# Moving the layer-norm work of the chunk two ahead one 128-token step sooner, in the two 16-head attention stages of a fused four-layer kernel

## The reference

```
L0: x += g * attn16x64(ln(x)*(1+sc)+sh);   x += g * gelu_mlp(ln(x)*(1+sc)+sh)
L1: x += g * attn16x16(rms(x)*w*(1+sc)+sh) # q, k normed per head, 3d rope
    x += g * swiglu_mlp(...)
L2: x += g * attn16x16(ln(x)*(1+sc)+sh)    # biases, rope over 64 positions
    x += g * gelu_mlp(...);  x += gelu(v)*tanh(g) @ W
L3: x += low-rank products with gelu
norm in front of an attention or MLP:
  m = mean(x); d = x - m                   (L1: no mean, d = x)
  v = mean(d*d); h = d / sqrt(v + eps) * (1 + scale) + shift
attention, within each sequence of 64 tokens:
  softmax(q k^T / sqrt(head size)) v @ W_out + b_out
```

## Time and profile before

| | us |
|---|---|
| median of three runs (2367.0 to 2367.68) | 2367.48 |
| the profiled execution's own time | 2364.86 |
| its span, first to last instruction | 2363.1 |
| TensorE matmul busy | 2005.7 (85%) |
| VectorE busy | 1455.1 (62%) |
| ScalarE busy | 968.7 (41%) |
| GpSimd busy | 835.4 (35%) |
| idle of PE ahead of the q, k projection L1378, in the page's groups | 78.3, of it 63.6 until HL (L588) |

### The profile page before, as it was taken

The page is one execution under the profiler, slowest core; times in us unless marked ns, Lnnn a source line. Parts: engine busy times, 40 slices in busy tenths (PEclk is TensorE's granted clock), DMA queues, the critical chain, the costliest instruction groups (busy, mean ns, idle before and its releaser), DMA issues. The chain is left out here.

```text
span 2363.1 us, 41380 instructions
## 1 busy us (share of the span) xinstructions
PE 2005.7 (85%) x15274; PEld 1565.9 (66%) x15274; DVE 1455.1 (62%) x2120; ACT 968.7 (41%) x1594; POOL 835.4 (35%) x759
## 2 busy tenths in 40 slices
PE   4829999999999799867787679997877877998998
PEld 4618878878887577646565567774655656777775
DVE  1236655656566455468888856775777774554554
ACT  0024434434444566534454433332333345664332
POOL 0041111211011344456665723345656572443000
PEclk9959999999999999978999989998998999999999
DMA  7120000000000100010000000001000000000001
GB/s 301 55 74 2 2 2 1 1 2 1 1 1 10 49 0 0 0 41 2 0 0 0 1 25 0 0 1 36 1 0 0 0 2 27 0 0 32 5 0 72
DMA packets 19519, 44.28 MB, mean 19 GB/s; under 512 B 3200, under 2 KB 11200, under 8 KB 18176
## 3 DMA queue, kind: packets, MB, share of 16 engines
q1 hardware_dynamic: 19392, 42.48, 5.1%
HBM read 36.18 MB, written 6.29 MB: 18 GB/s over the span
## 5 line engine op out<-in xcount | busy, mean ns | idle before, releaser
L1223 DVE TENSOR_TENSOR Glb<-Gfb,Ghb 128x512 fp32r<-128x512 f32 x176 | 168.2, 964 | 101.6 <-ACT Ghb L1176 100.0
L523 POOL TENSOR_TENSOR Tm<-Dv,MOD 128x512 f32<-128x512 f32 x96 | 111.3, 1179 | 298.6 <-DVE Dv L580 208.0
L633 PE MATMUL bank<-HH,W1b 128*128 128x512 f32 x448 | 183.8, 410 | 13.2 <-PEq L1493 6.9
L633 PE MATMUL O<-Ghb,W2b 128*128 128x512 f32 x352 | 144.1, 409 | 54.0 <-DVE Glb L1223 52.4
L634 PE MATMUL bank<-HL,W1b 128*128 128x512 f32 x448 | 177.2, 396 | 0.0
L635 PE MATMUL bank<-HH,W1b 128*128 128x512 f32 x448 | 176.9, 395 | 0.0
L1378 PE MATMUL bank<-WQKa,HH 128*128 128x512 f32 x256 | 101.4, 483 | 78.3 <-DVE HL L588 63.6
L653 POOL TENSOR_TENSOR spare<-RT 128x1 f32<-128x1 f32 x48 | 9.5, 197 | 446.0 <-DVE RT L644 446.0
L512 POOL TENSOR_TENSOR XS<-Tm 128x512 f32<-128x512 f32 x48 | 70.5, 1469 | 245.6 <-ACT Tm L478 245.6
L635 PE MATMUL O<-Ghb,W2b 128*128 128x512 f32 x352 | 138.4, 393 | 0.0
L634 PE MATMUL O<-Glb,W2b 128*128 128x512 f32 x352 | 137.8, 392 | 0.0
(11 more groups left out here) (244 smaller groups left out, 5470.0 us busy)
## 6 DMA issues: line engine op xcount, KB each, us to landing
w<-l_w_dram SPq DMA_DIRECT2D x4, 2048.0 KB, 26.7
wm<-w_mods_dram SPq DMA_DIRECT2D x6, 768.0 KB, 12.1
X<-xT_dram SPq DMA_DIRECT2D x4, 1024.0 KB, 36.3
out_dram<-XO SPq DMA_DIRECT2D x8, 512.0 KB, 2.7
W2b_f<-l_w_dram SPq DMA_DIRECT2D x11, 256.0 KB, 5.0
WQK_f<-l_wqk_dram SPq DMA_DIRECT2D x8, 256.0 KB, 7.1
W1b_0f<-l_w_dram SPq DMA_DIRECT2D x8, 256.0 KB, 3.5
b2r<-l_b2r_dram SPq DMA_DIRECT2D x1, 1024.0 KB, 7.7
```

The source lines that it names most:

```text
L523: nc.gpsimd.tensor_tensor(Tm[:, k].rearrange("p (b t) -> p b t", t=T), Dv[:, k].rearrange("p (b t) -> p b t", t=T), m, ALU.mult).then_inc( ...
L633: nc.tensor.matmul(out, w_lo_ap, x_hi, start=first, stop=False)
L1223: nc.vector.tensor_tensor(Gl[m % gb][:], gf, Gh[m % gb][:].bitcast(F32), ALU.subtract).then_inc(g_lo.h, 1)
```

## The change

In `attention12` alone, on all engines. For chunk c + 2: mean, d, square and ss stand at t = 1 (mean behind weights-times-v on PE, d behind OT on DVE); sqh and sql at t = 2; var (behind S) and v at t = 3; rstd, norm and pool_h at the end of t = 3, norm behind OT on DVE; HH and HL at the end of the tail, HL behind OL and ahead of the residual. Chunk 1, for which the norm starts ahead of the loop, gets pool_h, HH and HL at the end of the first step. The last chunk no longer has its own places: the next stage's chunk 0 is finished in chunk 6's tail, and its chunk 1 goes up to v at t = 3 of chunk 7, in the usual bank (`nf.var_bank` goes). No instruction of the engines is added or taken away, no DMA is touched, and the number of waits stays but for two that fall with the special cases.

```diff
@@ TensorE
-                            if not more:                      # in project_rest
-                                pe.wait_ge(s_sub.h, s_sub.at(NT))
-                                nf.var_bank = S2[:, 0, :]
-                                nf.pe_var(pe, 1)
...
                                 last.then_inc(s_ready.h, 1)
-                            if t == 2:
+                            if t == 3:
                                 f, cc = early(fr, nf, c, more)
-                                f.pe_mean(pe, cc)
-                            if tail and more:
-                                f, cc = early(fr, nf, c - 1, more)
                                 f.pe_var(pe, cc)
...
                                 weigh(pe, tt - 1, prev)
+                            if t == 1:
+                                f, cc = early(fr, nf, c, more)
+                                f.pe_mean(pe, cc)
                             if tail:
                                 pe.wait_ge(ot_hi.h, ot_hi.at(tt - 2)); pe.wait_ge(ot_lo.h, ot_lo.at(tt - 2))
-                                f, cc = early(fr, nf, c - 1, max(more, 1))
-                                pe.wait_ge(f_v.h, f.at(f_v, cc + 1 if more else 1))
+                                f, cc = early(fr, nf, c - 1, more)
+                                pe.wait_ge(f_v.h, f.at(f_v, cc + 1))
                                 project(1, 0)
@@ ScalarE
-                            if t == (1 if more else 3):       # ahead of q_t, oh and exp
-                                f, cc, pp = late(fr, nf, c, p, more)
-                                f.act_hh(act, cc, pp)
-                            if more and t == 3:
-                                f, cc = early(fr, nf, c, more)
-                                f.act_sqh(act, cc)
-                            if not more and tail:
-                                nf.act_sqh(act, 1)
...
-                            if t == (2 if more else 3):       # at the step's end
-                                f, cc = early(fr, nf, c, more)
+                            f, cc = early(fr, nf, c - 1 if tail else c, more)
+                            if t == 1:
                                 f.act_square(act, cc)
-                            if more == 2 and tail:
-                                fr.act_rstd(act, c + 1)
-                            if not more and t == 1:
-                                nf.act_rstd(act, 0)
+                            if t == 2:
+                                f.act_sqh(act, cc)
+                            if t == 3 and more:
+                                f.act_rstd(act, cc)
+                            if tail and more:
+                                f.act_hh(act, cc, 1 - p)
...
                         step(0, 0, 0, 2, first=True)
+                        fr.act_hh(act, 1, 1)
@@ VectorE
-                            if tail and more:                 # behind S less its maximum
-                                f, cc = early(fr, nf, c - 1, more)
+                            if t == 3:
+                                f, cc = early(fr, nf, c, more)
                                 f.dve_v(dve, cc)
...
-                            if t == (1 if more else 3):       # behind spread_k and ol
-                                f, cc, pp = late(fr, nf, c, p, more)
-                                f.dve_hl(dve, cc, pp)
-                            if t == (2 if more else 3):
-                                f, cc = early(fr, nf, c, more)
-                                f.dve_d(dve, cc)
...
                             if tail:
                                 ol(tt - 1, prev)
-                            if more == 2 and tail:
-                                fr.dve_norm(dve, c + 1)
-                            if not more and t == 1:
-                                nf.dve_norm(dve, 0)
+                            f, cc = early(fr, nf, c - 1 if tail else c, more)
+                            if t == 1:
+                                f.dve_d(dve, cc)
+                            if t == 3 and more:
+                                f.dve_norm(dve, cc)
+                            if tail and more:
+                                f.dve_hl(dve, cc, 1 - p)
...
-                            if not more:                      # in residual
-                                nf.var_bank = S2[:, 0, :]
-                                nf.dve_v(dve, 1)
...
                         fr.dve_norm(dve, 1)
+                        fr.dve_hl(dve, 1, 1)
@@ GpSimd, behind pool_rope
-                            if not more and t == 2:
-                                nf.pool_h(pool, 0, 0)
-                            f, cc = early(fr, nf, c, more)
-                            if t == (2 if more else 3):
+                            f, cc = early(fr, nf, c - 1 if tail else c, more)
+                            if first:
+                                fr.pool_h(pool, 1, 1)
+                            if t == 1:
                                 f.pool_ss(pool, cc)
+                            if t == 2:
+                                f.pool_sql(pool, cc)
                             if t == 3 and more:
-                                f.pool_sql(pool, cc)
-                            if not more and tail:
-                                nf.pool_sql(pool, 1)
-                            if more == 2 and t == 0:
-                                fr.pool_h(pool, c + 1, 1 - p)
+                                f.pool_h(pool, cc, p)
```

More of the change, by code:

```diff
@@ L1692, in _ @@
                     def _(dve):
-                        nf.var_bank = O2[:, 1, :]
                         dve.wait_ge(step_p.h, step_p.at(2 * TL))
```

## The result

| | before, us | changed, us |
|---|---|---|
| median (lowest to highest) | 2367.24 (2361.16 to 2367.68), 4 runs | 2333.93 (2330.18 to 2336.78), 4 runs |
| the profiled execution's own time | 2364.86 | 2335.44 |
| its span | 2363.1 | 2333.6 |
| mean granted TensorE clock | 0.946 | 0.955 |

The ratio is 0.9858, with a 95% interval of 0.9836 to 0.988: 33 us faster. The prediction was 46 us less for the profiled execution and a median of 2321. The two profiled executions differ by 29.4 us.

What follows compares the result with a forecast made beforehand. PE's waits for HL in t = 1 and long tails bound it, plain steps DVE (L1) or PE (L2). Periods -15.6 and -22.2, starts +3 and +1, ends -7.5 and -5 gave -46.3 us: 2318.6, median 2321, range 2308 to 2335.

Steps and rivals of the forecast that it cites:

- t = 1: Projection no longer waits for HL: L1's step 7.1 us, 6.5 less; L2's 8.3 us, 5.1 less.
- t = 2: Step loses the mean and the low clock: -1.9 us in L2, -0.8 in L1.
- t = 3 and tail: Taken as one piece, longer by the norm ahead of the tail's maximum: +4.4 us in L1, +2.7 in L2.
- HH and HL free: At the tail's end HH and HL cost nothing, since DVE has 4.5 us and more before t = 1's work.
- The clock: Half clock behind the tail's new PE stall of about 4 us costs 1.5 us a chunk, bounds 0 and 5.25.
- Six periods: Chunks of 40.9 us in L1 and 38.6 in L2 against means 43.5 and 42.3: -15.6 and -22.2 us.
- The starts: Each stage's first chunk pays the longer tail, its wait only moved: +3 us in L1, +1 in L2.
- Ends: Last chunk loses the next stage's norm, PE's longest KB waits, HH and HL: -7.5 us in L1, -5 in L2.
- B: Rival: the norm in t = 3 meets POOL's rope and stretches, 1.9 us a chunk, 23 us worse, 2344; chance 0.15.
- the signs that the prediction had named for being wrong: t = 1 keeps over 10 us, tail piece grows over 7 us, or t = 3's norm operations exceed 1 us.
- A: Rival: the tail's stall leaves PE's clock up, no clock loss, 18 us better, 2303; chance 0.14.
- C: Rival: tail's stall puts half clock on projections and S; slower beyond 5.4 us a period, 2380 at 6.5; chance 0.06.

Runs made afterwards that it cites:

- the third experiment: The changed kernel with HH and HL alone put back into t = 1, norm and pool_h staying early: 2354.11 us.
- the filled kernel: The changed kernel with repeated output-projection matmuls in PE's idle time in each tail, four more in L1 and three more in L2: 2337.85 us.
- the PT experiment: The changed kernel, but in L1's tails ACT copies PT ahead of the two root operations of SS: 2347.91 us.
- L2 alone: The change in the second 16-head stage only, the first built as in the kernel before: 2343.54 us.
- The first experiment: The changed kernel with norm and pool_h of chunk 1 ahead of the first step in both 16-head stages: 2320.81 us.
- The early half: Run alone on the kernel before: the pieces up to v one step sooner; rstd, norm, pool_h, HH and HL where they were: 2355.82 us.

## Why the prediction was right, and where its terms were off

The sign, the mechanism and the range held, the range by little: 2333.93 lies 1 us inside the forecast's own bound of 2335. The forecast of 2321 was 13 us under the measured median, and that it wasn't further off is in part luck, since L2's periods won 1.9 us more than their term. Step by step:

- *t = 1.* Right. No projection in the loop waits for HL; 7.8 (7.1 predicted) and 8.27 (8.3) us. The 0.7 in L1 is the plain step of the earlier trace rows, read at PE, where single steps scatter.
- *t = 2.* 6.8 in L2, as predicted; 7.8 in L1, the same misreading.
- *t = 3 and tail.* 9.37 + 16.15 against 7.11 + 13.67 is +4.7 in L1, where 4.4 and 1.5 for the clock were predicted; 7.85 + 14.78 against 6.74 + 12.55 is +3.3 in L2, where 2.7 and 1.5 were. The wait for OT came in L2 (3.0 us) and in L1 at another place, ahead of L1511, because on ACT the roots stand ahead of PT: with PT first the wait there fell from 3.63 to 0.33 us.
- *HH and HL free.* Right but for 0.4 us in L1: without them, in the third experiment, its tails take 13.8 us between maxima instead of 14.2. "Without that cover HL would be worth up to 2.3 us a chunk" was too low for L1, where it cost some 20 us in six periods, and too high for L2, where it cost 3.5.
- *The clock.* 1.3 us a chunk in L2 by the filled kernel, 1.5 predicted. In L1 it costs nothing: the periods of the filled kernel without a low stretch are as long as those with one (41.20 and 41.17). The stretch, 1203.5 to 1206.5, ends before the transpose that waits for OT (1207.99). That PE's low clock can cost there once it lies on the projections, the PT experiment shows.
- *Six periods.* I set the plain chunk of 40.9 us against a mean of 43.5 that holds one long period, the sixth, in which the weights are prepared. In L1 the first five took 43.0 each and now 41.0: the chunk's length was right and its gain too large, 2.1 and not 2.6. The sixth went only from 45.6 to 45.0. This rests on one trace of before: in "L2 alone" the same L1 code took 44.2 for each of the first five, so L1's gain may be larger than the table shows. The working also changed its yardstick: by its own parts and clock term the chunk was to lose 1.4 us in L1 and 2.8 in L2, while the sum took 2.6 and 3.7 against the mean. The chunks cut above lost 1.2 and 3.7. In L2 five went from 42.2 to 37.8 and the sixth from 42.5 to 40.7; the gain was 1.9 us larger in all than predicted.
- *The starts.* The term that was mis-sized most. "Its wait is only moved" was priced at +3 and +1 and cost 6.3 and 7.6 (in L2 4 to 8, by five traces). I had looked at when HH comes, not at what stands behind it: in the kernel before, ACT and DVE did a good part of step t = 1 beside pool_h, and now they do it after. The first experiment gave all of it back.
- *Ends.* -4.8 for -5 in L2, -5.1 for -7.5 in L1; the waits for KB went as said.
- *Rivals.* B came at a small part of its price: in L2 and for three of the four norm operations in L1 it's 0.69 us as before, but L1's first, L572, takes 1.01 to 1.14 in six of seven chunks. It stands beside the rope's last operation on POOL, which runs from 1195.14 to 1196.17 (timeline of DVE ahead of the tail of 1196.28). That is 0.3 us a chunk where B had 1.9, but by the letter it is one of the signs that the prediction had named for being wrong, over 1 us where it was 0.69:

```profile
1195.70 1.02 DVE L572 SCALAR_TENSOR_TENSOR V<-V 128x512 f32<-128x512 f32 x1
1196.75 0.69 DVE L574 TENSOR_TENSOR V<-V,V 128x512 f32<-128x512 f32 x1
...
1198.33 1.23 DVE L584 TENSOR_TENSOR Dv<-X,V 128x1024 f32<-128x1024 f32 x1 [0.16 <-DVE V L576]
```

A fell in L2, where a stall of 3.0 us is followed by 3.5 us at 0.52; in L1 the low stretch came and cost nothing. The early half, which the prediction treated as neutral but for t = 2, is about half of L2's gain in the six periods, by the mean that fills PE's wait for HL. The sum holds this, since it put the mean's 1.9 us down to t = 2; what it missed is that this part needs no early HL.
- *Slips that move nothing.* C turns at 64/12 = 5.3 us a chunk, not 5.4. Forecast, A and B together have 0.91, and their range is called 8 in 10. HL's longest in the earlier trace rows, 2.31 us, is in the MLP between the stages; in the attention stages it is 2.23. The 34 us for L2 don't follow from DVE's 32.0 but fit PE's 201.83/6 = 33.6.

## What to carry to other kernels

When a step is moved ahead in a queue, ask at the loop's start as well what is queued behind it on each engine, not only when its input comes. Read a stage's plain period at the engine that paces it, and over all periods one by one, before a mean is compared with a single chunk. A stall can be cheap where it stands: shortening one that lies ahead of unimportant work may only lengthen the next, which lies ahead of the work that counts.

## What the runs showed of the hardware

- Stalls of PE of 3.0 and 3.6 us, once a tail, are followed by one stretch of 3.0 to 3.5 us at 0.50 to 0.52; one of 5.5 us goes with 6.5 us at 0.50, which starts while PE still waits. With waits of at most 1.0 us the clock stayed at 1.00 for 160 us in L2, and with waits of at most 2.3 us for 95 us in L1 (1225 to 1320 of the filled kernel). The longest stall isn't all that counts: in the same kernel a wait of 2.0 us (at 1128.06) was followed by 6.5 us at 0.50.
- What a low stretch costs depends on what it lies on: in L2, on PE's projections, 1.3 us a chunk; in L1, under work that waits for DVE, nothing (41.20 us without it, 41.17 with it).
- Repeated matmuls in a wait are free where they fit into it (12.01 us of PE work instead of 11.43 in a tail that got 1.1 us shorter). In two L1 tails ahead of the loop's jump they came with waits of PE of 1.00 and 2.55 us that the profile puts down to no engine.
